# ScalarE copies the next block's transposes ahead of the second half of an expert block

## The reference

```
logits = x @ router_weight.T + router_bias              # 2048 rows, 8 experts
topk_logits, topk_idx = top_k(logits, 4)
combine = softmax(topk_logits) at topk_idx, 0 elsewhere
gate, up = split(x @ gate_up_proj[e].T + gate_up_bias[e])   # 512 columns each
gate = min(gate, 7); up = clip(up, -7, 7)
act = (up + 1) * gate * sigmoid(1.702 * gate)
out[e] = act @ down_proj[e].T + down_bias[e]
y = sum over e of out[e] * combine[:, e];  x = x + y
```

## Time and profile before

| | before |
|---|---|
| median of three runs | 1025.26 us |
| profiled execution | 1030.46 us, span 1028.7 us |
| busy over the span | TensorE 781.0 us (76%), VectorE 641.2 (62%), ScalarE 489.6 (48%), GpSimd 282.9 (28%) |
| line 1570, `gate_up` on TensorE | 1872 matmuls, 28.9 us idle ahead of them until ScalarE's `xt` |
| line 1479, clip on VectorE | 78, 95.4 us idle ahead of them until ScalarE's `up` |
| chain that ended last | ScalarE 15% of the span, VectorE 13%, issue 6%, TensorE 2% |

### The profile page before, as it was taken

The page is one execution under the profiler, slowest core; times in us unless marked ns, Lnnn a source line. Parts: engine busy times, 40 slices in busy tenths (PEclk is TensorE's granted clock), DMA queues, the critical chain, the costliest instruction groups (busy, mean ns, idle before and its releaser), DMA issues. The chain is left out here.

```text
span 1028.7 us, 18106 instructions
## 1 busy us (share of the span) xinstructions
PE 781.0 (76%) x6136; PEld 498.5 (48%) x6136; DVE 641.2 (62%) x1238; ACT 489.6 (48%) x950; POOL 282.9 (28%) x261
## 2 busy tenths in 40 slices
PE   0682666678858798888777753999899998999893
PEld 0341323232424242432332242888787887888782
DVE  4536655877687778867779427555565555555552
ACT  1110300454414654366668511466666666666662
POOL 5004000310030000000000001355565555655543
PEclk9865556778977999898697565799999999999997
DMA  8411462014321331115353203133333333333332
GB/s 269 124 51 41 131 160 79 32 42 124 89 67 53 119 99 32 53 58 189 98 181 125 63 22 113 43 50 60 61 63 54 59 59 64 59 56 60 59 43 31
DMA packets 72070, 83.19 MB, mean 81 GB/s; under 512 B 10288, under 2 KB 65200, under 8 KB 71856
## 3 DMA queue, kind: packets, MB, share of 16 engines
q1 hardware_dynamic: 57008, 61.25, 19.4%
q0 software_dynamic: 14976, 20.78, 12.6%
HBM read 52.71 MB, written 29.29 MB: 80 GB/s over the span
## 5 line engine op out<-in xcount | busy, mean ns | idle before, releaser
L1570 PE MATMUL gu_ps<-xt,w 128*128 128x256 f16 x1872 | 214.2, 275 | 28.9 <-ACT xt L1291 28.9
L1570 PEld LDWEIGHTS gu_ps<-xt,w 128*128 (+1 forms) x1872 | 180.9, 99 | 61.9 <-issue 39.3
L672 ACT ACTIVATE p<-st 128x512 f32<-128x512 f32 x256 | 138.8, 595 | 123.2 <-PE st L1137 122.6
L883 DVE TENSOR_REDUCE neg_max<-sc 128x2 f32<-128x1024 f32 x128 | 156.3, 1221 | 63.3 <-PE sc L1116 62.5
L1361 POOL DMA_INDIRECT out<-y,block_rows x78 | 125.2, 1605 | 138.9 <-ACT y L1321 117.6
L1584 PE MATMUL dn_ps<-w,h 128*128 (+1 forms) x936 | 108.6, 273 | 1.4 <-DVE h L1488 1.4
L1479 DVE TENSOR_SCALAR up<-up 128x512 f32<-128x512 f32 x78 | 42.5, 544 | 96.1 <-ACT up L1307 95.4
L1353 POOL DMA_INDIRECT gx<-xr_d,block_rows x78 | 86.2, 1105 | 52.0 <-DVE block_rows L1461 29.1
L1116 PE MATMUL sc<-kz,sq 48*128 48x512 f16 x256 | 63.5, 468 | 43.1 <-DVE neg_max L883 38.2
L1584 PEld LDWEIGHTS dn_ps<-w,h 128*128 128x128 f16 x936 | 89.9, 98 | 11.4 <-issue 1.6
L1150 PE MATMUL pv<-p,v 128*17 128x512 f32 x512 | 81.5, 716 | 5.8 <-ACT p L672 5.8
(11 more groups left out here) (194 smaller groups left out, 1064.2 us busy)
## 6 DMA issues: line engine op xcount, KB each, us to landing
stack_d<-t SPq DMA_DIRECT2D x16, 256.0 KB, 2.4
raw<-in_gate_up_t SPq DMA_DIRECT2D x4, 1024.0 KB, 5.2
raw_next<-in_gate_up_t SPq DMA_DIRECT2D x4, 1024.0 KB, 5.3
sq<-stack_d SPq DMA_DIRECT2D x16, 192.0 KB, 3.4
kz<-stack_d SPq DMA_DIRECT2D x16, 192.0 KB, 4.4
sq<-stack_d SPq DMA_DIRECT2D x32, 96.0 KB, 3.3
kz<-stack_d SPq DMA_DIRECT2D x32, 96.0 KB, 3.2
ctx_pad<-in_ctx SPq DMA_DIRECT2D x4, 512.0 KB, 4.0
```

Source lines behind the costliest of these rows:

```text
L672: act.activation(p32[:, n // 2 % RING, 2 * (n % 2) + i, :], st[:, i, :], ACT.Exp, scale=QSCALE).then_inc(s_exp, 1)
L883: dve.tensor_reduce(neg_max[:, qt, :, pair], sc[:], AX.X, ALU.max, negate=True).then_inc(m_max, 1)
L1570: ins = pe.matmul(gu_ps[:, 2 * half + g, q * ROWS:(q + 1) * ROWS], weights(i, wi, slice(col, col + P)), xt[:, i % 2, kd, xi, :], start=(j ...
```

## The change

In each turn of its loop, ScalarE now makes the copy `take_x(i + 2)` after `high_half(2i + 2)` and ahead of `unit(2i + 3)`; before, it stood behind that unit and ahead of `high_half(2i + 3)`. No instruction is added or taken away, and the lists of the other engines are as they were.

```diff
@@ -1335,9 +1335,9 @@
                 if i + 1 < NB:
                     unit(2 * i + 2)
                     high_half(2 * i + 2)
-                    unit(2 * i + 3)
                     if i + 2 < NB:
                         take_x(i + 2)
+                    unit(2 * i + 3)
                     high_half(2 * i + 3)
                 scale_y(i)
```

## The result

The changed kernel is slower. Its four runs took 1061.97, 1062.05, 1063.23 and 1801.3 us; the last of these is disturbed and left out of the ratio, but the median of 1062.64 us counts it (1062.05 without it). The ratio to the kernel before is 1.0338, 95% interval 1.0295 to 1.038. The kernel before, with a fourth run of 1035.12 us beside the three known ones, has its median at 1026.03 us, so the medians are 36.6 us apart (36.0 by 1062.05). The profiled execution took 1063.23 us (span 1061.4), against 1030.46 before.

What follows compares the result with a forecast made beforehand. The prediction took a ring of waits between ScalarE and VectorE, not TensorE, to bound the kernel. An uncovered copy of 0.945 us in 37 turns adds 35.0 us to the median 1025.26, giving 1060.3 us, range 1054 to 1067.

Steps and rivals of the forecast that it cites:

- The ring: Expert loop: ScalarE and VectorE wait for each other in turn and set the 9.13 us turn; TensorE is in no link.
- Nothing removed: Second half of a turn: `h` waits about 1.22 us for `prod` instead of 0.31; earlier `xt` gains nothing.
- The price of a copy: Between first `h` and second `glu`: the uncovered copy adds 0.945 us a turn, bounds 0.92 to 1.07, 37 times.
- Covered waits: At the moved copy: the transposes end 0.6 us before ScalarE gets there, so the copy does not wait for them.
- TensorE's wait: TensorE waiting for `xt`: 10.07 - 8.52 = 1.55 us a turn, some 57 us in all, against 28.9.
- Sum and level: Whole run: 37 x 0.945 = 35.0 us, added to the timed median 1025.26, 5.2 us below the profiled execution.
- The clips: VectorE's clips beside GpSimd's stores and gathers: 0.68 us first, 0.43 us second, taken as unchanged by the move.
- The clock: TensorE's granted clock: expected to stay at 1.00 (2.4 GHz) throughout the loop.
- TensorE as the bound: Rival for the loop: earlier `xt` takes TensorE's wait away, 29 us faster, 996 us; chance 4%.
- a delay swallowed ahead of `y`: Rival at ScalarE's 1.36 us idle before `y`: a later `h` costs nothing, 1025 us; chance 3%.
- a slowed second clip: Rival on VectorE: the second clip meets a gather, 9.3 us more, 1069.6 us; chance 4%.
- The rival of a lower clock: Rival on TensorE: longer waits lower its clock, 136 us more, 1161 us; chance 2%.

## Why the prediction was right

The forecast was 1060.3 us (1054 to 1067). The time was 1062.6, the difference 36.6 us where 35.0 were forecast. The mechanism and the price hold. That 34.4 us belong to the move, so near to 35.0, is in part luck: a copy costs 0.92 us and not 0.945 in 36 turns, and the first turn costs 1.4.

- **The ring.** Right. TensorE's work taken away in the kernel before (0.87 us) or added in the changed one (0.89 us) moved no turn in the middle of the loop, and reordering ScalarE's list, then VectorE's too, gained 17 and 36 us in the medians.
- **Nothing removed.** Right. The second `h` waits 1.22 us behind `up`, to the hundredth as worked out. The earlier `xt` gained nothing.
- **The price of a copy.** Right with a small error: 0.92 us instead of 0.945. In its new place the copy lasts 1.006 us in the median, not 1.039, and `glu` starts 0.10 us before it ends (815.88 + 1.01 against 816.79). The upper bound of 1.07 us came from a row that was read wrongly. The `h` at 656.86 was not held by the copy alone: it needs `prod`, and VectorE's row below ends at 656.82. `h` starts 0.04 us behind `prod`, exactly as in the middle of the loop (815.35 and 815.39), so this pair says nothing of how closely two ScalarE instructions follow each other. Leaning on the lower rows was right.
- **Covered waits.** Right in the middle of the loop, wrong in its first turn, where TensorE is the late one after filling up: the copy waited 0.76 us for the transposes there, and the turn lost 1.4 us.
- **TensorE's wait.** Forecast 1.55 us a turn and some 57 in all; the trace has 1.57 and 56.3. But the work that I subtracted, 8.52 us a turn, was wrong in itself: back to back it is 8.30. A wait in this view runs from the modelled end of the last matmul, while without a wait the next starts before that end (at 798.91 in the run with more transposes, where 793.67 + 5.40 = 799.07), so real slack is larger than the wait shown, by about 0.2 us here.
- **Sum and level.** 34.4 us between the two traces belong to the move. Between the medians lie 36.6, within what the interval allows (30 to 39 us), and the 2 us beyond 34.4 are no part of the mechanism. Adding 35.0 to the timed median, not to the profiled execution, was sound, but where the 5.2 us between the two lie was never shown: no timed run has a trace. That loops repeat closely from trace to trace (342.24, 342.44, 342.80 us in three of them) while their first `y` moves by 9 us suggests that they lie ahead of the loop.
- **The clips.** Right: 0.43 us in the second half, 0.68 in the first, as before.
- **The clock.** I had said 1.00 throughout the loop. That was wrong, without a cost, as the last section shows.

VectorE's timeline of the kernel before, the `prod` ahead of the `h` at 656.86:

```profile
656.13 0.69 DVE L1483 SCALAR_TENSOR_TENSOR prod<-glu,up 128x512 f32<-128x512 f32 x1
```

The row of line 1291 over the changed kernel's whole run (ns min/median/max, starts, forms), which gives the 1.006 us:

```profile
L1291 ACT ACTIVATE xt<-tr_ps x39: 1006/1006/1024, 636.9 to 1029.2; 128x1024 f16<-128x1024 f16 x39
```

Of the rivals, TensorE as the bound is ruled out by the runs that gave it less or more to do, and by the one where `xt` came earlier still and the turn stayed at 9.13 us; a delay swallowed ahead of `y` by the unchanged 48.9 us of that wait; and a slowed second clip by its duration. The rival of a lower clock did set in, in three turns, and cost nothing.

## What to carry to other kernels

An instruction on an in-order engine costs what the wait behind it doesn't cover. Look at what its engine waits for after it, not at who wants its result early: the same copy cost 0, 0.92 and 0 us a turn in three neighbouring places. The busiest engine (TensorE, 90% here) needn't be the bound; a ring of two engines that hand a tile back and forth can hold it up, and doing both halves before waiting for the other loosens the ring (here by 1.9% on ScalarE alone, by 3.9% on both), until the busiest engine really is the bound.

## What the runs showed of the hardware

**The clock fell in some turns whose wait was long.** In the kernel before, the granted clock was 1.00 through the middle of the loop, with no wait above 1.71 us. In the changed one it fell to the lower level (1.2 GHz, 0.50 from 869 to 871 us) three times. Its TensorE timeline in one of these, and a window around it (busy as above; the clock is the number before the last two):

```profile
868.31 6.92 PE L1570 MATMUL gu_ps<-xt,w 128*128 128x256 f16 x48 [2.61 <-ACT xt L1291]
```

```profile
735.00:799.00 64.00, 53.39 (x504) 46.66 (x505) 32.59 (x75) 37.42 (x82) 35.56 (x26) 1.00 0.35 56
864.00:874.00 10.00, 7.39 (x55) 5.79 (x54) 5.20 (x12) 5.95 (x14) 5.56 (x4) 0.83 0.34 55
```

Each time TensorE had waited 2.0 to 2.6 us just before, in a turn lengthened by VectorE's loads; the waits of 1.57 us in the other turns left the clock alone, and three of the six long waits did too. The 48 matmuls took 6.9 to 7.1 us instead of 5.41, and the turn stayed at 10.04, since TensorE had 1.7 us to spare. The changed kernel with the copy made twice has more long waits: behind 14 of its 23 waits of 2.2 us or more the matmuls took 6.7 to 7.1 us, and its turns still stayed at 10.98. In the kernel with a shorter down product it happened behind two of six waits of 1.95 us or more (at 745.42 and 912.54, 7.08 us each). There `up` had to wait 0.71 us for its bank, and the turn took 9.80 us instead of 9.14: idle time on an engine off the ring can come back as 0.7 us on it. I did not test what exactly lets the clock fall.

**A gather slows when a clip has just begun.** GpSimd's second gather took 1.27 us in the changed kernel, 0.08 us behind the start of the clip, and 1.08 before; over the whole run a gather took 1192 ns on average, against 1105. The other traces bear it out. Every gather of the changed kernel and of its variant with more transposes that began 0.07 to 0.10 us into a clip took 1.25 to 1.27 us, 58 in all from 690 to 960 us. With both units first on ScalarE, those 0.15 to 0.17 us into a clip took 1.22 or 1.23. The gathers of the kernel before, none of which began in a clip, took 1.06 to 1.11. It cost nothing here, for the turn grew by the copy alone. No run was made to separate the clip from what else runs at that moment.
